# Centering a feed-forward tile before the previous tile's way up, with two center banks and two way-up banks

## What is computed

```python
x = x + mixer(x)                            # 2-D Fourier mixer, down product by w2
y = layernorm(x)                            # over the 24 channels
h = relu(q_acc(q_acc(q_mul(y) @ q_mul(W1).T) + q_mul(b1)))   # 24 -> 96
x = x + q_acc(q_acc(q_mul(h) @ q_mul(W2).T) + q_mul(b2))     # 96 -> 24
```

## Time and profile before

| | us |
|---|---|
| median of 3 runs | 4319.72 (4318.26 to 4321.03) |
| the profiled execution | 4321.37 |
| its span, first to last instruction | 4319.7 |
| mean granted TensorE clock | 0.938 of full speed |
| PE busy | 3681.6 (85%) |
| PE weight loads busy | 2510.3 (58%) |
| DVE busy | 1767.9 (41%) |
| ScalarE busy | 1843.0 (43%) |
| GpSimd busy | 232.0 (5%) |

### The profile page before, as it was taken

One profiled execution on the slowest core, in us unless ns is written; L12 is line 12 of the kernel. 1 busy time (PEld: TensorE's weight loads), 2 busy tenths in 40 slices (PEclk: granted clock), 3 DMA queues, 4 the chain that ended last, 5 costly groups with the idle time before them and its releaser, 6 DMA issues.

```text
span 4319.7 us, 131667 instructions
## 1 busy us (share of the span) xinstructions
PE 3681.6 (85%) x55580; PEld 2510.3 (58%) x55580; DVE 1767.9 (41%) x2885; ACT 1843.0 (43%) x3483; POOL 232.0 (5%) x489
## 2 busy tenths in 40 slices
PE   3988879988798888988889979889788897899887
PEld 2647646467455674556745647546566475564755
DVE  3523454234543345334353344533445234452344
ACT  1453444433454334444345444453443534435344
POOL 3400000000000000000000000000000000000000
PEclk7999999999899999899999999899999999999989
DMA  4201001010010100101001010010100101001000
GB/s 120 51 22 27 2 14 27 16 27 3 14 27 16 26 3 14 27 16 27 3 14 41 2 26 3 15 41 2 26 3 15 40 2 26 12 6 25 18 11 13
DMA packets 24223, 88.72 MB, mean 21 GB/s; under 512 B 17843, under 2 KB 18211, under 8 KB 19643
## 3 DMA queue, kind: packets, MB, share of 16 engines
q1 hardware_dynamic: 22339, 74.72, 7.2%
q0 software_dynamic: 1280, 5.21, 0.4%
HBM read 63.86 MB, written 14.84 MB: 18 GB/s over the span
## 4 chain that ended last, share of the span: by engine, by line
PE 74%; ACT 8%; DVE 6%; issue 6%; SPq 3%; DMA 2%; ACTq 0%; DVEq 0%
PE ps L986 74%; ACT rs L605 3%; ACT lv L600 3%; DVE area_ty L822 2%; DMA area_ty<-area_hz 2%; SPq L429 1%; SPq L412 1%; DVE xs L955 1%; ACT sq L592 1%; DVE area_hz L843 0%; DVE area_ty L927 0%; DVE area_hz L925 0%; DVE area_ty L951 0%; ACT area_ty L646 0%; ACT area_ty L650 0%
## 5 line engine op out<-in xcount | busy, mean ns | idle before, releaser
L822 DVE TENSOR_TENSOR area_ty<-ps,rs 128x448 f32<-128x448 f32 (+2 forms) x416 | 285.1, 685 | 633.1 <-ACT rs L605 633.1
L986 PE MATMUL ps<-area_hz 32*64 32x147 f32 (+2 forms) x7180 | 376.8, 296 | 84.2 <-DVE area_hz L843 31.3
L986 PE MATMUL ps<-area_ty,area_hz 113*64 113x49 f32 (+1 forms) x10240 | 403.4, 253 | 44.8 <-DMA area_ty<-area_hz 41.1
L703 ACT ACTIVATE area_ty<-ps 120x448 f32<-120x448 f32 (+1 forms) x448 | 243.8, 544 | 450.7 <-PE ps L986 450.7
L927 DVE COPY area_ty<-ps 120x448 f32<-120x448 f32 (+1 forms) x432 | 270.0, 625 | 399.5 <-PE ps L986 399.5
L703 ACT ACTIVATE area_hz<-ps 112x384 f32<-112x384 f32 (+2 forms) x384 | 191.4, 498 | 531.6 <-PE ps L986 531.6
L986 PEld LDWEIGHTS ps<-area_ty,area_hz 113*64 113x64 f32 (+1 forms) x10240 | 339.5, 137 | 122.2 <-issue 119.3
L986 PE MATMUL ps<-sq,keep_sb 128*128 128x448 f32 (+1 forms) x832 | 382.4, 562 | 26.7 <-ACT sq L592 26.6
L986 PEld LDWEIGHTS ps<-area_hz 32*64 32x64 f32 (+2 forms) x7180 | 297.0, 160 | 181.3 <-issue 152.5
L986 PE MATMUL ps<-area_ty,wconv 128*128 128x448 f32 x1008 | 398.0, 539 | 0.1
L986 PE MATMUL ps<-keep_sb,area_hz 112*56 112x56 f32 (+1 forms) x12288 | 367.7, 222 | 14.7 <-DVE area_hz L925 13.8
(11 more groups left out here) (106 smaller groups left out, 4219.0 us busy)
## 6 DMA issues: line engine op xcount, KB each, us to landing
area_hz<-f_all SPq DMA_DIRECT2D x16, 2541.0 KB
xw<-x_in SPq DMA_DIRECT2D x8, 1568.0 KB, 6.8
y_out<-xs SPq DMA_DIRECT2D x32, 294.0 KB
f_all<-piece POOLq DMA_DIRECT2D x16, 317.6 KB, 3.4
area_ty<-area_hz SPq DMA_DIRECT2D x256, 4.6 KB
area_hz<-raw_in SPq DMA_DIRECT2D x1, 2894.0 KB, 9.3
g_sb<-g_in SPq DMA_DIRECT2D x2, 1396.5 KB
g_sb<-g_in SPq DMA_DIRECT2D x1, 1470.0 KB
```

Source lines behind the costliest of these rows:

```text
L703: act.activation(dst, src, ACT.Relu if st in (ST_H, ST_F2) else ACT.Copy).then_inc(sc_kept, 1)
L822: ve.tensor_tensor(o, a, b, ALU.mult, **kw).then_inc(normed, 1)
L986: return pe.matmul(o, a, b, start=start, stop=stop)
```

## The change

- `center_bank` gives the feed-forward tiles two banks, 0 for even tiles and 6 for odd ones. By `user_before` a tile's center then waits for the scaling of the tile two back.
- The way up has two banks, 4 + m % 2. The third matmul (m = 2) writes bank 4 again and waits for the copy of the first (m = 0) of its own tile: `f_half` at k * HC + 1. The first two wait for the last copies of their banks in the tile in front.
- On PE the center of tile s comes before the way up of tile s-1 and behind the way down of tile s-2.
- On ScalarE the square of tile s comes before the three copies of tile s-1.

Nothing is added or removed in the arithmetic, and no DMA is changed.

```diff
--- before.py
+++ after.py
@@ -134,7 +134,9 @@
         return 4 + i % 4
     if which == LN_CONV:
         return i % 2
-    return {LN_MIX(0): 4, LN_MIX(1): 1, LN_WIN1: 1}.get(which, 0)
+    if which in (LN_FFN(0), LN_FFN(1)):
+        return (0, 6)[i % 2]
+    return {LN_MIX(0): 4, LN_MIX(1): 1, LN_WIN1: 1}[which]
 
 
 def variance_bank(k):
@@ -718,16 +720,16 @@
                             act.wait_ge(f_bias, q * 2 * NT + k - 1)
                         act.activation(o16[:, s % 2, :], ps[:, 7, 0:TT], ACT.Copy
                                        ).then_inc(f_out, 1)
+                    if s < NT:
+                        square(q, LN_FFN(l), s)
                     if 0 <= s - 1 < NT:
                         k = l * NT + s - 1
                         for m in range(HC):
                             act.wait_ge(f_up, (q * 2 * NT + k) * HC + m + 1)
                             if m == 0 and s - 1 >= 2:
                                 act.wait_ge(f_relu, (q * 2 * NT + k - 1) * HC)
-                            act.activation(a16[:, (s - 1) % 2, m, :], ps[:, 4 + m, 0:TT], ACT.Copy
+                            act.activation(a16[:, (s - 1) % 2, m, :], ps[:, 4 + m % 2, 0:TT], ACT.Copy
                                            ).then_inc(f_half, 1)
-                    if s < NT:
-                        square(q, LN_FFN(l), s)
                     if l == 0 and 0 <= s - 2 < NT:
                         square(q, LN_MIX(1), s - 2)
                     if l == 1 and s < NW:
@@ -1307,19 +1309,21 @@
                             ins = mm(ps[:, 7, 0:TT], ffn2[:, l, m, :], hq8[:, i % 2, m, :],
                                      start=m == 0, stop=m == HC - 1)
                         ins.then_inc(f_down, 1)
+                    if s < NT:
+                        pe.wait_ge(ve_kept, q * VE_FILLS + vector_fills(step_of(l, ST_FFN, s) + 1))
+                        center(q, LN_FFN(l), s, xs)
                     if 0 <= s - 1 < NT:
                         i = s - 1
                         k = q * 2 * NT + l * NT + i
                         pe.wait_ge(normed, ln_count(q, LN_AT[LN_FFN(l), i]))
                         for m in range(HC):
-                            if i >= 1:
-                                pe.wait_ge(f_half, (k - 1) * HC + m + 1)
+                            if m == 2:
+                                pe.wait_ge(f_half, k * HC + 1)
+                            elif i >= 1:
+                                pe.wait_ge(f_half, (k - 1) * HC + 3 - m)
                             pe.sem_inc(passed_pe, 1)
-                            mm(ps[:, 4 + m, 0:TT], ffn1[:, l, m, :], xq8[:, TT * i:TT * i + TT]
+                            mm(ps[:, 4 + m % 2, 0:TT], ffn1[:, l, m, :], xq8[:, TT * i:TT * i + TT]
                                ).then_inc(f_up, 1)
-                    if s < NT:
-                        pe.wait_ge(ve_kept, q * VE_FILLS + vector_fills(step_of(l, ST_FFN, s) + 1))
-                        center(q, LN_FFN(l), s, xs)
                     if l == 0 and 0 <= s - 2 < NT:
                         pe.wait_ge(ffn_added, q * 2 * NT + s - 1)
                         center(q, LN_MIX(1), s - 2, xs)
```

## The result

The changed kernel takes 4329.66 us (median of 20 runs, 4317.93 to 4341.67), the kernel before 4319.41 us in as many runs beside it. The ratio is 1.0026, with an interval from 1.0015 to 1.0038: some 11 us slower. The direction was forecast, the size was not: 4343 with a range from 4330 to 4360.

What follows compares the result with a forecast made beforehand. TensorE's work bounds the kernel, but hand-over rings bound the feed-forward slots. Layer 1's 21.0 us plus layer 0's 2.6 made 23.6 us, put on the 4319.72 us median: 4343 us, range 4330 to 4360.

Steps and rivals of the forecast that it cites:

- The two rings: Hand-over cycles setting a feed-forward slot: layer 1 from 6.39 to 6.76 us; layer 0 level, 0.03 us more a slot.
- the path through ScalarE: Feed-forward slot: the square ahead of the copies delays each copy by one ScalarE step, 0.43 us.
- the hand-over from the copy to the third matmul: Feed-forward slot: delay from the first way-up copy's end to the third way-up matmul, taken as 0.25 us.
- The low end of 0.21: Lowest value allowed for the delay from copy end to third way-up matmul, in us; with no 0.10, period 6.62.
- the 0.10 for a start after an idle stretch: Third way-up matmul to window center: 0.10 us more behind idle PE, so 0.29 in place of 0.19.
- the tail of layer 1: Slot 7 of layer 1, without feed-forward center or square: 0.67 us lost a quad, all paid to the quad's end.
- Slot 1: Layer 1's first slot, no way-down copy queued: third matmul about 0.1 us late, between 0 and 0.37.
- the step into slot 7: Layer 1, last of slots 2 to 6, each forecast 0.37 us longer.
- the long ring: Layer 1 slot period after the change, 6.76 us against 6.39, counted for five slots: 1.85 us a quad.
- layer 0's start: Layer 0, slot 2: way down 0.31 us late, next down-mix 0.2; layer 0 in all 0.3 a quad, 2.6 us.
- Rival (c): Clock also falls to half in layer 1's sparser tail: 11 us more in 8 quads, 4354 us; chance 0.08.
- rival (b): Wait real but short, with hand-over 0.05 and no 0.10: layer 1 period 6.46, time 4326 us; chance 0.09.

## Why the prediction was right and wrong

- **Right: what bounds a slot.** The two rings were read correctly. The center went into the hole, and the new wait for the copy came onto the path in layer 1. In layer 0 it did not.
- **Right: the path through ScalarE.** The prediction had the way-down copy, square and first copy at 2.13, 2.55 and 2.98 us behind the Ln; measured 2.13, 2.56 and 2.98.
- **Wrong: the hand-over from the copy to the third matmul**, put at 0.25. The first copy starts at 587.24 and lasts 0.546 (the mean of L731), the matmul starts at 587.93: 0.145. The rows I had were not of this kind: the 0.25 followed a DVE write, and the 0.33 a ScalarE copy that was wanted as weights. The low end of 0.21 had no row at all, and the measured value lies between it and the lowest row listed, 0.05.
- **Wrong: the 0.10 for a start after an idle stretch.** The center follows the third matmul by 0.19, not 0.29. I read it from the lengths of two merged groups (0.83 and 0.73), where it lies inside the group and isn't paid again. Nor does it come from idling. In slot 1 of layer 0 of the kernel before, where the way-up matmuls have no wait for a copy, the group takes 0.73 behind 2.17 us of idle PE (the line below). Taken one by one, way-up matmuls start 0.19 apart without such a wait and 0.24 with it, and two steps with it are the 0.10. With both terms right the ring is 6.76 - 0.105 - 0.10 = 6.55, which is what was measured. These two terms are the mis-sized step: 0.21 too much in each of 40 slots, 8.4 us.

```profile
416.18 0.73 PE L986 MATMUL ps<-area_ty,ffn 128*128 128x448 fp8e5 x3 [2.17 <-DVE area_ty L822]
```

- **Wrong: the tail of layer 1.** From the Ln of the last tile to the last add it is 7.85 against 7.43, 0.42 more where 0.67 was forecast, by the same two terms. And one gain was missed. In slot 7 there is no down-mix between the last center and the variance, so before the change the variance waited for ScalarE's square, which stood behind the copies. PE's weight loads and matmuls there, before:

```profile
595.98 0.82 PE L986 MATMUL ps<-xw,keep_sb 128*128 128x392 f32 x2
...
596.81 0.30 PEld L986 LDWEIGHTS ps<-sq,keep_sb 128*128 128x128 f32 x2 [0.63 <-ACT sq L592]
```

```profile
594.66 0.82 PE L988 MATMUL ps<-xw,keep_sb 128*128 128x392 f32 x2
595.32 1.67 PE L988 MATMUL ps<-sq,keep_sb 128*128 128x448 f32 x4
```

  Before, the variance follows the last center by 0.83 and was released by L592; now by 0.66. That and the next Ln give 0.12 back. Slot 1 gives 0.09 where 0.1 of loss was forecast: the center had stood on the path there too. In sum: slot 1 -0.09, four full slots +0.57 (25.62 to 26.19), the step into slot 7 -0.12 (5.58 to 5.46), the tail +0.42, together the measured 0.78 a quad, against 2.6 forecast. I had counted the step into slot 7 as a fifth slot on the long ring; it is the one that turned shorter.
- **Wrong: layer 0's start.** The way down of slot 2 was late, by 0.20 where 0.31 was forecast (9.24 behind the first center against 9.04), but the Ln of that slot was not (14.89 against 14.91): the early center had given as much back. 0 in place of 2.6 us.
- **Not forecast at its place: the clock.** Rival (c) had it in the tail of layer 1, with 11 us. It is there in ten of the sixteen quads profiled, with 0.8 us each (50.7 against 49.90) where rival (c) had 1.4, and before the change in two of sixteen; but the larger part is in layer 0's tail, where the kernel before was already at the edge. That row was in front of me, and I took it as given instead of asking what the change would do to it.

So of the 23.6 us forecast 6.2 came from the order of the work. The 17.4 too much are 8.4 from the two terms in the slots, 2.8 from the step into slot 7 and the rest of the ring, 2.0 from the tail of layer 1, 1.5 from slot 1 and 2.6 from layer 0. The other 5 of the 11 measured go with the clock, as far as the profiles and the mean clocks show. By the order alone the time would have been some 4326 us, which is the figure of rival (b), and for much of its reasons: a shorter hand-over and no 0.10. That the result came within 0.4 us of the range is luck: the clock, which the sum did not have, brought it there.

The rule of the Trainium skill (Perfetto Trace Analysis, § Optimizing Tensor Performance, Matmuls) that independent groups should rotate through different PSUM banks is borne out here with a price: the third bank is worth 0.95% (4329.7 to 4288.4 us), and taking it from the kernel before costs 58 us. The advice of the Trainium skill to find the gaps on the engine in question and let what they wait for start sooner stands in the same page's § Optimization Strategy. Here it paid in time only once the bank was there.

## What to carry to other kernels

When a matmul is moved into a hole, ask which buffer pays for it, and walk the ring again with the new wait in it: here the hole of 1.04 us was filled and one of 0.85 opened behind the copy. Before giving up a bank, look for one whose last reader is done by the time of the write, even if it serves something else. In a pipeline written out by hand cost the first and the last slots by themselves; their ring is another one, and here the sign turned over in the step into slot 7.

## What was not expected of the hardware

A ScalarE copy's recorded end to a matmul that waits for it, with a counter increment between, is 0.145 us, against 0.25 from DVE's fp8 write (580.88 + 0.62 to 581.75). Way-up matmuls in a row start 0.19 us apart, and 0.24 apart where the later one has a wait of its own, though what it waits for is long done. The granted clock fell to 1.2 GHz in layer 0's tail of the first quad of the kernel before although PE had no idle stretch over 1.1 us in the 6 us ahead of it: in the 3.5 us before the stretch of the fall it was busy for 1.85. And keeping PE busy there with matmuls that nobody reads made the kernel before 0.42% faster, with 18.4 us for the tail in every quad.
